# The token list of a mixture-of-experts stage: eight units' row one-hots by one comparison, and ScalarE on the block side of every fourth unit

## The chip, the cores and the metric

The kernel runs on one core of a Trainium2 chip. The metric is the device time of one execution in microseconds (us): the median of the timed runs, lower is better.

## The reference, cut to what matters

One decoder layer on 64 sequences of 256 tokens, 256 features: a quantised self-attention, a cross-attention, and a third block with its own attention and a mixture of eight experts. Only the mixture matters here. T = 16384 tokens; each goes to its two best experts, each expert has C = 4096 places, and a token that comes too late is dropped:

```python
top1 = jnp.argmax(probs, axis=-1)
...
top2 = jnp.argmax(jnp.where(m1 > 0, -jnp.inf, logits), axis=-1)
...
loc1 = jnp.cumsum(m1, axis=0) - 1.0
loc2 = jnp.cumsum(m2, axis=0) - 1.0 + m1.sum(0, keepdims=True)
m1 = m1 * (loc1 < C)
m2 = m2 * (loc2 < C)
...
buf = buf.at[top1, s1].set(x, mode='drop')
buf = buf.at[top2, s2].set(x, mode='drop')
h = jax.nn.relu(jnp.einsum('ecd,edf->ecf', buf, w1) + b1[:, None, :])
```

## The kernel before, in words

The program is a sequence of stages with a barrier of all engines between two of them: `prepare`, three times `attention` (kinds A, X, F), `route`, `dispatch`, `experts`. The stage that the change touches is `dispatch`, some 95 us of the program.

`route` has left, for each of the 128 x 128 tokens (partition p, column n) and each of its two choices i, a slot number between 0 and 32767 (8 experts x 4096 places), split into `high` (slot / 128, 0 to 255) and `low` (slot modulo 128). `dispatch` turns this round: for each slot it finds the token that sits there, as a table `token` of 128 rows x 256 columns, which `experts` reads for its gathers.

It does so by matmuls of one-hot matrices. A **unit** u is one column n and one choice i (n = u // 2, i = u % 2), 256 units in all. For each unit the kernel makes a row side, 128 x 128 in bf16, with a 1 where the column number equals the token's `low`, and a block side, 128 x 256 in bf16, with the token's code where the column number equals its `high`. TensorE multiplies them (row side as the weights, block side as the moving operand of 256 columns) and adds all 256 products in one PSUM tile `code_sum` of 128 x 256.

- VectorE makes both sides of 214 units, with one TENSOR_SCALAR each (L1366 for `by_row`, one comparison; L1367 for `block_of`, a comparison and a product). Each has six buffers, R = 6.
- ScalarE makes both sides of every sixth unit (42 units, SHARE = 6), with two ACTIVATEs for each side: Abs of the distance (`row_gap` L1383, `block_gap` L1384), then Relu of one minus it (`row_a` L1396, `block_a` L1397). Two buffers each, RA = 2. The gaps of the next ScalarE unit are issued ahead of the shapes of this one.
- TensorE takes the units in their number's order (L1411) and waits for each one's sides.
- Before the loop VectorE makes the codes and their negatives, step by step (L1349 to L1359), and turns GpSimd's column numbers (L1342) into bf16 (L1361). ScalarE starts when the thirteenth of these steps is done.
- Behind the loop VectorE waits for the last matmul, copies the sum out (L1370) and makes the token numbers (L1371 to L1374). Then the stage ends.
- The DMA queue of SyncE writes the gates (`tail`) to memory meanwhile (L1336) and waits for that.

The order on each engine is written out by hand; no planner is in it. The lines that bind the engines are:

```python
if d >= R:
    dve.wait_ge(summed, ON_DVE[d - R] + 1)
...
if a >= RA:
    act.wait_ge(summed, ON_ACT[a - RA] + 1)
...
dve.wait_ge(summed, U)
chain.step(v.tensor_copy(codes[:, :], code_sum[:, :]))
```

Of the kernel before, what the change touches and what calls it, by code (L numbers as in the profile page):

```python
# [68 lines left out]
def allocators(nc, ctx, prefix):  # L69
    def sb(name, shape, dtype=F32):  # L70
        return ctx.enter_context(nc.sbuf_tensor(prefix + name, shape, dtype))

    def ps(name, shape, dtype=F32):
        return ctx.enter_context(nc.psum_tensor(prefix + name, shape, dtype))

    sems = []

    def sem(name):
        sems.append(nc.alloc_semaphore(prefix + name))
        return sems[-1]  # L80
# [1224 lines left out]
def dispatch(nc, C, D, io, scratch):  # L1305


    NT, CAP = D["T"] // P, D["CAP"]
    HI = NE * CAP // P
    R, RA = 6, 2  # L1310
    U = 2 * NT
    SHARE = 6
    BIAS = 127 - NT // 2
    with ExitStack() as ctx:
        sb, ps, sem = allocators(nc, ctx, "disp_")
        column, columns = sb("column", [P, HI], I32), sb("columns", [P, HI], BF16)
        place, power = sb("place", [P, NT], I32), sb("power", [P, NT], I32)
        row1, unit = sb("row1", [P, 1]), sb("unit", [P, 1])
        code, code_minus = sb("code", [P, NT]), sb("code_minus", [P, NT])
        low_minus, high_minus = [[sb(f"{n}{i}", [P, NT]) for i in range(2)] for n in ("low_minus", "high_minus")]  # L1320
        by_row, block_of = ([sb(f"{n}{k}", [P, m], BF16) for k in range(R)] for n, m in (("by_row", P), ("block_of", HI)))
        row_gap, block_gap = ([sb(f"{n}{k}", [P, m]) for k in range(RA)] for n, m in (("row_gap", P), ("block_gap", HI)))
        row_a, block_a = ([sb(f"{n}{k}", [P, m], BF16) for k in range(RA)] for n, m in (("row_a", P), ("block_a", HI)))
# [3 lines left out]
        numbered, link, built, spaced, shaped, summed, tail_out = (  # L1327
            sem(n) for n in ("numbered", "link", "built", "spaced", "shaped", "summed", "tail_out"))
        ON_ACT = [u for u in range(U) if u % SHARE == SHARE - 1]
        ON_DVE = [u for u in range(U) if u % SHARE != SHARE - 1]  # L1330
        powers = power[:, :].bitcast(F32)

        with nc.Block() as block:
            @block.sync
            def _(sp):
                sp.dma_start(scratch["h2"].rearrange("(n p) f -> p n f", p=P)[:, :, 256:259], C["tail"][:, :, :],  # L1336
                             allow_slow_non_contiguous=True).then_inc(tail_out, 16)
                sp.wait_ge(tail_out, 16)

            @block.gpsimd  # L1340
            def _(pool):
                nc.gpsimd.iota(column[:, :], [[1, HI]], base=0, channel_multiplier=0).then_inc(numbered, 1)  # L1342
                pool.wait_ge(numbered, 1)

            @block.vector
            def _(dve):
                v = nc.vector
                chain = Chain(dve, link, 0, 18, C["passed"])
                chain.step(v.tensor_scalar(place[:, :], C["number"][:, :], 7, None, ALU.logical_shift_right))  # L1349
                chain.step(v.tensor_scalar(place[:, :], place[:, :], BIAS, None, ALU.add))  # L1350
                chain.step(v.tensor_scalar(power[:, :], place[:, :], 23, None, ALU.logical_shift_left))
                chain.step(v.tensor_copy(row1[:, :], C["number"][:, 0:1]))
                chain.step(v.tensor_scalar(row1[:, :], row1[:, :], 1.0 / P, 1.0, ALU.mult, ALU.add))
                chain.step(v.tensor_scalar(code[:, :], powers, row1[:, :], None, ALU.mult))
                chain.step(v.tensor_scalar(code_minus[:, :], code[:, :], -1.0, None, ALU.mult))
                chain.step(v.memset(unit[:, :], 1.0))
                for i in range(2):
                    chain.step(v.tensor_scalar(low_minus[i][:, :], C["low"][i][:, :], -1.0, None, ALU.mult))
                    chain.step(v.tensor_scalar(high_minus[i][:, :], C["high"][i][:, :], -1.0, None, ALU.mult))  # L1359
                dve.wait_ge(numbered, 1)  # L1360
# [12 lines left out]
                chain.step(v.tensor_scalar(nothing[:, :], number[:, :], 0.0, float(2 ** 20), ALU.is_equal, ALU.mult))  # L1373
                chain.step(v.scalar_tensor_tensor(C["token"][:, :], number[:, :], -float(P * BIAS), nothing[:, :], ALU.add,  # L1374
                                                  ALU.add))
                chain.close()

            @block.scalar
            def _(act):
                def gaps(a):  # L1380
# [7 lines left out]
                gaps(0)  # L1388
                for a, u in enumerate(ON_ACT):
                    n, k = u // 2, a % RA  # L1390
                    if a + 1 < len(ON_ACT):
                        gaps(a + 1)
                    act.wait_ge(spaced, a + 1)
                    if a >= RA:
                        act.wait_ge(summed, ON_ACT[a - RA] + 1)
                    nc.scalar.activation(row_a[k][:, :], row_gap[k][:, :], ACT.Relu, bias=unit[:, :], scale=-1.0)  # L1396
                    nc.scalar.activation(block_a[k][:, :], block_gap[k][:, :], ACT.Relu, bias=code[:, n:n + 1],  # L1397
                                         scale=code_minus[:, n:n + 1]).then_inc(shaped, 1)

            @block.tensor  # L1400
            def _(pe):
                for u in range(U):
                    if u in ON_ACT:
                        a = ON_ACT.index(u)
                        pe.wait_ge(shaped, a + 1)
                        row, blocks = row_a[a % RA], block_a[a % RA]
                    else:
                        d = ON_DVE.index(u)
                        pe.wait_ge(built, d + 1)
                        row, blocks = by_row[d % R], block_of[d % R]  # L1410
                    nc.tensor.matmul(code_sum[:, :], row[:, :], blocks[:, :], start=u == 0, stop=u == U - 1).then_inc(summed, 1)  # L1411

# [554 lines left out]
```

## Time and profile before

| | |
|---|---|
| median of 3 runs | 5688.54 us (5688.51 to 5694.07) |
| profiled execution, its own time | 5689.64 us |
| its span, first to last instruction | 5687.9 us |
| TensorE / VectorE / ScalarE busy, share of the span | 93% / 79% / 65% |
| granted TensorE clock, mean of the span | 0.974 |

"Busy" is the time in which an engine had an instruction running. Matmul records overlap, because matmuls are pipelined and their ends are modelled, so a share of 93% is not 93% of what TensorE can do. In a timeline the start of an instruction is its first number and its duration the second; on VectorE and ScalarE the next instruction can start before the one ahead has ended. "Idle before" is the time that the engine stood still ahead of an instruction, and the name behind the arrow is what ended it. The granted clock is a share of TensorE's full 2.4 GHz: 0.50 is its lower level of 1.2 GHz.

### The profile page before, as it was taken

The numbers are of one execution on the slowest core, as the hardware profiler recorded it, in microseconds if no ns is written. First come the engines' busy times: TensorE is split into PE (matmuls) and PEld (weight loads), VectorE is DVE, ScalarE is ACT, GpSimd is POOL, SyncE is SP. The second block draws the span as 40 slices with busy tenths as digits, with TensorE's granted clock in tenths as the row PEclk, the third lists the DMA queues.
The fourth block names the chain that finished last, engine by engine and source line by source line (L and its number), as shares of the span: only waits on it lengthen the run. The fifth ranks groups of instructions, "written<-read, shape, count | busy, mean of one in ns | idle before, by whom it ended". The sixth has DMA issues, their size and how long they took to land. (4 is left out here: it accounts for less than half of the span.)

```text
span 5687.9 us, 155750 instructions
## 1 busy us (share of the span) xinstructions
PE 5301.0 (93%) x47387; PEld 4213.5 (74%) x47388; DVE 4520.0 (79%) x12198; ACT 3673.0 (65%) x8251; POOL 2070.8 (36%) x1753
## 2 busy tenths in 40 slices
PE   0899999979999999799999999995899999999998
PEld 0677777757777777567777777761799999899997
DVE  7889998867777777588888888878777777677776
ACT  4788888858888888577777776764344444444443
POOL 0322222223344333244444444430344444344443
PEclk9999999989999999999999999995899999999999
DMA  5677777746666666466666666652222322222321
GB/s 157 173 183 184 183 184 183 183 124 185 184 186 184 184 183 186 122 168 180 178 168 180 178 169 178 179 144 6 65 57 42 57 50 44 53 47 43 58 41 26
DMA packets 631736, 751.04 MB, mean 132 GB/s; under 512 B 143363, under 2 KB 560332, under 8 KB 631472
## 3 DMA queue, kind: packets, MB, share of 16 engines
q1 hardware_dynamic: 575136, 679.62, 45.9%
q0 software_dynamic: 49152, 63.10, 6.9%
q10 hardware_dynamic: 7184, 5.00, 0.4%
q8 instruction: 142, 2.33, 0.2%
q14 instruction: 122, 1.00, 0.1%
HBM read 476.49 MB, written 272.24 MB: 132 GB/s over the span
## 5 line engine op out<-in xcount | busy, mean ns | idle before, releaser
L1853 POOL DMA_INDIRECT out_dram<-exp_gated,exp_token x256 | 425.6, 1662 | 890.1 <-DMA out_dram<-exp_gated,exp_token 325.5
L831 ACT ACTIVATE F_probs<-F_scoreT 128x512 f32<-128x512 f32 x1024 | 585.8, 592 | 233.7 <-PE F_scoreT L658 233.3
L940 DVE TENSOR_REDUCE F_tops<-F_score 128x2 f32<-128x512 f32 x1024 | 684.0, 686 | 53.4 <-PE F_score L686 36.3
L940 DVE TENSOR_REDUCE A_tops<-A_score 128x3 f32<-128x384 f32 x1024 | 528.0, 553 | 64.3 <-PE A_score L676 56.3
L831 ACT ACTIVATE A_probs<-A_scoreT 128x384 f32<-128x384 f32 x1024 | 451.1, 488 | 28.7 <-PE A_scoreT L646 15.2
L658 PE MATMUL F_scoreT<-QS,KS 98*128 98x256 bf16 x2048 | 365.5, 275 | 9.7 <-ACT F_probs L831 1.5
L686 PE MATMUL F_score<-KS,QS 96*128 96x256 bf16 x2048 | 362.9, 274 | 8.8 <-DMA KS<-d_k 7.9
L1834 POOL DMA_INDIRECT exp_x<-d_h,exp_token x256 | 281.1, 1098 | 179.3 <-DMA exp_w<-in_L_ffn_w_dram 101.7
L1630 ACT ACTIVATE exp_hT<-exp_hT,exp_b 128x512 f32<-128x512 f32 x512 | 338.6, 711 | 3.1 <-DVE exp_hT L1785 3.1
L940 DVE TENSOR_REDUCE X_tops<-X_score 128x4 f32<-128x484 f32 x512 | 323.4, 653 | 15.7 <-PE X_score L681 14.5
L831 ACT ACTIVATE X_probs<-X_scoreT 121x512 f32<-121x512 f32 x512 | 297.2, 588 | 31.4 <-PE X_scoreT L654 28.6
L671 PE MATMUL A_score<-causal,ident_b 128*128 128x256 bf16 x1024 | 283.7, 277 | 12.4 <-DMA KS<-d_k 8.5
L823 ACT ACTIVATE X_score<-X_mask 128x484 f32<-128x484 bf16 x512 | 288.3, 571 | 8.0 <-DVE X_tops L940 6.8
L642 PE MATMUL A_scoreT<-ident_b,causal 128*128 128x128 bf16 x2048 | 286.6, 221 | 3.1 <-ACT A_probs L831 1.3
L674 PE MATMUL A_score<-KS,QS 96*128 96x256 bf16 x1024 | 281.9, 275 | 0.0
L646 PE MATMUL A_scoreT<-QS,KS 98*128 98x256 bf16 x1024 | 277.7, 271 | 0.0
L712 PE MATMUL F_outs<-F_probs,V 128*32 128x256 f32 x4096 | 275.7, 387 | 1.9 <-ACT F_outT L840 1.9
L1664 ACT ACTIVATE exp_pair<-exp_lead 128x256 f32<-128x256 f32 x256 | 98.3, 384 | 264.7 <-PE exp_lead L1589 264.5
L658 PEld LDWEIGHTS F_scoreT<-QS,KS 98*128 98x128 bf16 x2048 | 164.2, 97 | 134.8 <-issue 51.9
L1655 ACT ACTIVATE exp_lone<-exp_lead 128x256 f32<-128x256 f32 x256 | 98.3, 384 | 242.3 <-PE exp_lead L1574 234.7
L1550 PE MATMUL exp_side_r<-exp_w2s,exp_hTs 128*128 128x128 f32 x2048 | 249.7, 275 | 0.0
L1110 POOL TENSOR_TENSOR A_left_q<-A_q_f,A_q_parts 128x512 f32<-128x512 f32 x64 | 74.1, 1158 | 473.4 <-ACT A_q_parts L905 473.4
(392 smaller groups left out, 16046.8 us busy)
## 6 DMA issues: line engine op xcount, KB each, us to landing
QS<-d_q SPq DMA_DIRECT2D x384, 192.0 KB, 3.7
KS<-d_k SPq DMA_DIRECT2D x256, 192.0 KB, 4.0
QS<-d_q SPq DMA_DIRECT2D x384, 128.0 KB, 3.9
KS<-d_k SPq DMA_DIRECT2D x256, 128.0 KB, 4.0
d_q<-A_q_parts SPq DMA_DIRECT2D x64, 384.0 KB, 3.5
d_k<-A_k_parts SPq DMA_DIRECT2D x64, 384.0 KB, 3.9
QS<-d_q SPq DMA_DIRECT2D x384, 64.0 KB, 3.6
d_q<-X_q_parts SPq DMA_DIRECT2D x64, 384.0 KB, 2.7
```

The costliest lines, as they stand in the source:

```text
L642: mm(s[:, n * P:(n + 1) * P], C["causal"][:, 0:P], ident_b[:, :], start=n == 0, stop=False, skip_group_check=True)
L646: last = mm(s[:, P:384], k[0:98, i, 0:P], q[0:98, i, :], start=False, stop=True, skip_group_check=True)
L658: last = mm(s[:, n * 256:(n + 1) * 256], k[0:98, i, n * P:(n + 1) * P], q[0:98, i, :], start=True, stop=True)
L671: mm(s[:, 0:384].rearrange("p (n k) -> p n k", n=3)[:, 0:3:2, :], ident_b[:, :], C["causal"][:, :].rearrange("p (n k) -> p n k", n=2), sta ...
L674: mm(s[:, P:384], q[0:96, i, P:256], k[0:96, i, :], start=False, stop=False, skip_group_check=True)
L686: last = mm(s[:, n * 256:(n + 1) * 256], q[0:96, i, n * P:(n + 1) * P], k[0:96, i, :], start=True, stop=True)
L823: nc.scalar.activation(score[i % SB][:, 0:2 * HB * KN].rearrange("p (u n k) -> p u n k", u=HB, n=2), mask[gp][:, :, 0:KN].unsqueeze(1).bro ...
L831: nc.scalar.activation(probs[m % 2][0:KR, at:at + HB, :].rearrange("p u x -> p (u x)"), scoreT[i % TB][0:KR, 0:HB * TCOL], ACT.Exp)\
L940: nc.vector.tensor_reduce(dst, src, AX.X, ALU.max).then_inc(score_read, 1)
L1630: nc.scalar.activation(hT[par][:, f, :], hT[par][:, f, :], ACT.Relu, bias=b1[k][:, f:f + 1])\
L1834: nc.gpsimd.indirect_dma_start(x[j % XB][:, s, :], None, scratch["h2"], bass.IndirectOffsetOnAxis(token[j % (2 * XB)][:, s:s + 1], 0), bou ...
L1853: nc.gpsimd.indirect_dma_start(out, bass.IndirectOffsetOnAxis(token[j % (2 * XB)][:, s:s + 1], 0), gated[par][:, s, :], None, bounds_check ...
```

## The change

The row side of eight units (G = 8) is now made by VectorE with one TENSOR_TENSOR comparison. Its first input `repeated` is a constant 128 x 1024 bf16 tile that holds every column number eight times in a row (made once, by a GpSimd iota and a conversion to bf16); its second is the eight units' `low` values, eight adjacent bf16 numbers per partition, read again for each of the 128 column numbers. The output has the eight units interleaved: column j of unit g is element 8 j + g. TensorE therefore reads a unit's weights with a step of 8 elements (16 bytes). There are three such tiles (RR = 3), and 32 such comparisons.

The block side is made per unit as before, by VectorE for 192 units (eight buffers, R = 8) and by ScalarE for every fourth (64 units, SHARE = 4, RA = 3). ScalarE makes no row sides any more. VectorE now waits for `summed` ahead of each comparison of rows and ahead of each block side; before it waited once per unit, ahead of the row side.

```diff
-    R, RA = 6, 2
-    U = 2 * NT
-    SHARE = 6
+    U, G, RR, R, RA = 2 * NT, 8, 3, 8, 3
+    N = U // G
+    SHARE = 4
...
+        spread_out, repeated = sb("spread_out", [P, P, G], I32), sb("repeated", [P, P, G], BF16)
...
+                nc.gpsimd.iota(spread_out[:, :, :], [[1, P], [0, G]], base=0, channel_multiplier=0).then_inc(numbered, 1)
...
-                chain.step(v.memset(unit[:, :], 1.0))
                 for i in range(2):
-                    chain.step(v.tensor_scalar(low_minus[i][:, :], C["low"][i][:, :], -1.0, None, ALU.mult))
+                    chain.step(v.tensor_copy(low[:, :, i], C["low"][i][:, :]))
...
                 chain.step(v.tensor_copy(columns[:, :], column[:, :]))
-                for d, u in enumerate(ON_DVE):
-                    n, i, k = u // 2, u % 2, d % R
-                    if d >= R:
-                        dve.wait_ge(summed, ON_DVE[d - R] + 1)
-                    v.tensor_scalar(by_row[k][:, :], columns[:, 0:P], C["low"][i][:, n:n + 1], None, ALU.is_equal)
-                    v.tensor_scalar(block_of[k][:, :], columns[:, :], C["high"][i][:, n:n + 1], code[:, n:n + 1],
-                                    ALU.is_equal, ALU.mult).then_inc(built, 1)
+                chain.step(v.tensor_copy(repeated[:, :, :], spread_out[:, :, :]))
+                d = 0
+                for k in range(N):
+                    if k >= RR:
+                        dve.wait_ge(summed, G * (k - RR + 1))
+                    lows = low[:, :, :].rearrange("p n i -> p (n i)")[:, G * k:G * k + G].unsqueeze(1).broadcast_to([P, P, G])
+                    v.tensor_tensor(by_row[k % RR][:, :, :], repeated[:, :, :], lows, ALU.is_equal).then_inc(rows_built, 1)
+                    for u in range(G * k, G * k + G):
+                        if u not in ON_DVE:
+                            continue
+                        if d >= R:
+                            dve.wait_ge(summed, ON_DVE[d - R] + 1)
+                        n, i = u // 2, u % 2
+                        v.tensor_scalar(block_of[d % R][:, :], columns[:, :], C["high"][i][:, n:n + 1], code[:, n:n + 1],
+                                        ALU.is_equal, ALU.mult).then_inc(built, 1)
+                        d += 1
...
-                    nc.scalar.activation(row_gap[k][:, :], columns[:, 0:P], ACT.Abs, bias=low_minus[i][:, n:n + 1])
                     nc.scalar.activation(block_gap[k][:, :], columns[:, :], ACT.Abs, bias=high_minus[i][:, n:n + 1])\
                         .then_inc(spaced, 1)
...
-                    nc.scalar.activation(row_a[k][:, :], row_gap[k][:, :], ACT.Relu, bias=unit[:, :], scale=-1.0)
...
                 for u in range(U):
+                    k = u // G
+                    if u % G == 0:
+                        pe.wait_ge(rows_built, k + 1)
...
-                    nc.tensor.matmul(code_sum[:, :], row[:, :], blocks[:, :], start=u == 0, stop=u == U - 1).then_inc(summed, 1)
+                    nc.tensor.matmul(code_sum[:, :], by_row[k % RR][:, :, u % G], blocks[:, :], start=u == 0, stop=u == U - 1)\
+                        .then_inc(summed, 1)
```

VectorE's order at the head of the loop, before; each row is an instruction, with its output and inputs and the output's size:

```order
L1358 TENSOR_SCALAR disp_low_minus<-low 128x128
L1359 TENSOR_SCALAR disp_high_minus<-high 128x128
L1361 CAST disp_columns<-disp_column 128x256
L1366 TENSOR_SCALAR disp_by_row<-disp_columns,low 128x128
L1367 TENSOR_SCALAR disp_block_of<-disp_columns,high,disp_code 128x256
L1366 TENSOR_SCALAR disp_by_row<-disp_columns,low 128x128
L1367 TENSOR_SCALAR disp_block_of<-disp_columns,high,disp_code 128x256
```

and now:

```order
L1358 CAST disp_low<-low 128x128
L1359 TENSOR_SCALAR disp_high_minus<-high 128x128
L1361 CAST disp_columns<-disp_column 128x256
L1362 CAST disp_repeated<-disp_spread_out 128x1024
L1368 TENSOR_TENSOR disp_by_row<-disp_repeated,disp_low 128x1024
L1375 TENSOR_SCALAR disp_block_of<-disp_columns,high,disp_code 128x256 x6
L1368 TENSOR_TENSOR disp_by_row<-disp_repeated,disp_low 128x1024
L1375 TENSOR_SCALAR disp_block_of<-disp_columns,high,disp_code 128x256 x6
```

A comparison of 1024 elements and six block sides have taken the place of the pairs, and one conversion of 1024 elements stands ahead of the loop.

ScalarE's order in the loop, before:

```order
L1383 ACTIVATE disp_row_gap<-disp_columns,disp_low_minus 128x128
L1384 ACTIVATE disp_block_gap<-disp_columns,disp_high_minus 128x256
L1396 ACTIVATE disp_row_a<-disp_row_gap,disp_unit 128x128
L1397 ACTIVATE disp_block_a<-disp_block_gap,disp_code,disp_code_minus 128x256
```

and now:

```order
L1392 ACTIVATE disp_block_gap<-disp_columns,disp_high_minus 128x256 x2
L1404 ACTIVATE disp_block_a<-disp_block_gap,disp_code,disp_code_minus 128x256
L1392 ACTIVATE disp_block_gap<-disp_columns,disp_high_minus 128x256
L1404 ACTIVATE disp_block_a<-disp_block_gap,disp_code,disp_code_minus 128x256
```

Two ACTIVATEs per ScalarE unit are left of four.

## Rows read from the trace of the kernel before

**Rows 1.** Busy time by stretch: in `route`, and the loop of `dispatch`

```profile
core 0: us, PE busy (x) PEld busy (x) DVE busy (x) ACT busy (x) POOL busy (x), PEclk, DMA share, GB/s
3873.00:3903.00 30.00, 2.25 (x5) 0.61 (x5) 26.64 (x63) 1.25 (x2) 0.00 (x0) 0.50 0.00 0
...
3907.40:3997.61 90.21, 85.71 (x256) 23.37 (x256) 89.72 (x428) 70.35 (x168) 0.00 (x0) 0.50 0.36 2
```

**Rows 2.** Waits, 3903 to 4002 us: us in total, times, longest

```profile
PEld disp_code_sum L1411 <- DVE disp_block_of L1367: 71.4, 214, 5.4
...
ACT disp_row_a L1396 <- PE disp_code_sum L1411: 13.7, 35, 1.2
```

**Rows 3.** Waits of the SyncE queue in the same stretch

```profile
SPq L1333 <- PEq L1333: 71.3, 1, 71.3
...
SPq L1333 <- DMA d_h<-tail: 24.1, 1, 24.1
```

**Rows 4.** Instructions on the row and block tiles: ns min/median/max, first and last start

```profile
L1366 DVE TENSOR_SCALAR disp_by_row<-disp_columns,low x214: 234/236/255, 3907.4 to 3996.6; 128x128 bf16<-128x128 bf16 x107
L1411 PEld LDWEIGHTS disp_code_sum<-disp_block_of,disp_by_row x214: 101/103/106, 3908.0 to 3997.2; 128*128 128x128 bf16 x107
...
L1367 DVE TENSOR_SCALAR disp_block_of<-disp_columns,high,disp_code x214: 327/329/341, 3907.6 to 3996.8; 128x256 bf16<-128x256 bf16 x107
```

**Rows 5.** Timeline of VectorE in the middle of the loop: start us, us

```profile
3950.13 0.23 DVE L1366 TENSOR_SCALAR disp_by_row<-disp_columns,low 128x128 bf16<-128x128 bf16 x1
3950.30 0.33 DVE L1367 TENSOR_SCALAR disp_block_of<-disp_columns,high,disp_code 128x256 bf16<-128x256 bf16 x1
3950.55 0.24 DVE L1366 TENSOR_SCALAR disp_by_row<-disp_columns,low 128x128 bf16<-128x128 bf16 x1
```

**Rows 6.** Groups by line, VectorE: busy us, mean ns of one

```profile
L1276 DVE TENSOR_SCALAR route_pos<-route_pos 128x128 f32<-128x128 f32 x1 | 0.2, 226 | 0.0
...
L1280 DVE TENSOR_TENSOR route_slot<-route_pos,route_base 128x128 f32<-128x128 f32 x1 | 0.3, 291 | 0.0
...
L1274 DVE TENSOR_TENSOR route_loc<-route_loc,route_one 128x1024 f32<-128x1024 f32 x2 | 2.5, 1225 | 0.1
...
L944 DVE COPY X_maskT<-X_mask 128x244 bf16<-128x244 bf16 x64 | 13.9, 218 | 0.0
```

**Rows 7.** Timeline of VectorE, two comparable instructions behind each other in `experts`

```profile
4010.60 0.68 DVE L1703 TENSOR_TENSOR exp_w1s<-exp_w 128x512 f32<-128x512 f32 x1
4011.20 0.68 DVE L1705 TENSOR_TENSOR exp_w1s<-exp_w1s,exp_w 128x512 f32<-128x512 f32 x1
```

**Rows 8.** Timeline ahead of the loop, at its start and at its end

```profile
3903.96 0.35 POOL L1342 IOTA disp_column<- 128x256 int32 x1 [49.91 <-POOLq L84]
...
3905.93 0.06 DVE L1356 MEMSET disp_unit<- 128x1 f32 x1
...
3907.40 0.26 DVE L1366 TENSOR_SCALAR disp_by_row<-disp_columns,low 128x128 bf16<-128x128 bf16 x1
...
3996.80 0.33 DVE L1367 TENSOR_SCALAR disp_block_of<-disp_columns,high,disp_code 128x256 bf16<-128x256 bf16 x1
3997.61 0.42 DVE L1370 COPY disp_codes<-disp_code_sum 128x256 f32<-128x256 f32 x1 [0.49 <-PE disp_code_sum L1411]
```

**Rows 9.** Timeline of ScalarE at the start of the loop

```profile
3908.40 0.49 ACT L1384 ACTIVATE disp_block_gap<-disp_columns,disp_high_minus 128x256 f32<-128x256 bf16 x1
3908.80 0.39 ACT L1396 ACTIVATE disp_row_a<-disp_row_gap,disp_unit 128x128 bf16<-128x128 f32 x1
...
3909.09 0.58 ACT L1397 ACTIVATE disp_block_a<-disp_block_gap,disp_code,disp_code_minus 128x256 bf16<-128x256 f32 x1
...
3909.71 0.40 ACT L1383 ACTIVATE disp_row_gap<-disp_columns,disp_low_minus 128x128 f32<-128x128 bf16 x1
```

**Rows 10.** Timeline of TensorE in `route`: matmuls of 512 columns, and a weight load

```profile
3873.93 0.64 PE L1225 MATMUL route_whole<-route_one,ones_b 128*128 128x512 bf16 x1
3874.36 0.64 PE L1224 MATMUL route_inside<-route_one,below 128*128 128x512 bf16 x1
...
3874.36 0.15 PEld L1225 LDWEIGHTS route_whole<-route_one,ones_b 128*128 128x128 bf16 x1 [0.28 <-issue]
```

More of the change, by code:

```diff
@@ L1316, in dispatch @@
         column, columns = sb("column", [P, HI], I32), sb("columns", [P, HI], BF16)
+        spread_out, repeated = sb("spread_out", [P, P, G], I32), sb("repeated", [P, P, G], BF16)
         place, power = sb("place", [P, NT], I32), sb("power", [P, NT], I32)
[L1318 to L1323, printed above, removed]
+        row1, code, code_minus = sb("row1", [P, 1]), sb("code", [P, NT]), sb("code_minus", [P, NT])
+        low, high_minus = sb("low", [P, NT, 2], BF16), [sb(f"high_minus{i}", [P, NT]) for i in range(2)]
+        by_row = [sb(f"by_row{k}", [P, P, G], BF16) for k in range(RR)]
+        block_of = [sb(f"block_of{k}", [P, HI], BF16) for k in range(R)]
+        block_gap, block_a = ([sb(f"{n}{k}", [P, HI], t) for k in range(RA)] for n, t in (("block_gap", F32), ("block_a", BF16)))
         codes, number, nothing = sb("codes", [P, HI]), sb("number", [P, HI]), sb("nothing", [P, HI])
@@ L1326, in dispatch @@
         code_sum = ps("code_sum", [P, HI])
-        numbered, link, built, spaced, shaped, summed, tail_out = (
-            sem(n) for n in ("numbered", "link", "built", "spaced", "shaped", "summed", "tail_out"))
+        numbered, link, rows_built, built, spaced, shaped, summed, tail_out = (
+            sem(n) for n in ("numbered", "link", "rows_built", "built", "spaced", "shaped", "summed", "tail_out"))
         ON_ACT = [u for u in range(U) if u % SHARE == SHARE - 1]
@@ L1342, in _ @@
                 nc.gpsimd.iota(column[:, :], [[1, HI]], base=0, channel_multiplier=0).then_inc(numbered, 1)
-                pool.wait_ge(numbered, 1)
+                nc.gpsimd.iota(spread_out[:, :, :], [[1, P], [0, G]], base=0, channel_multiplier=0).then_inc(numbered, 1)
+                pool.wait_ge(numbered, 2)
             @block.vector
@@ L1355, in _ @@
                 chain.step(v.tensor_scalar(code_minus[:, :], code[:, :], -1.0, None, ALU.mult))
-                chain.step(v.memset(unit[:, :], 1.0))
                 for i in range(2):
-                    chain.step(v.tensor_scalar(low_minus[i][:, :], C["low"][i][:, :], -1.0, None, ALU.mult))
+                    chain.step(v.tensor_copy(low[:, :, i], C["low"][i][:, :]))
                     chain.step(v.tensor_scalar(high_minus[i][:, :], C["high"][i][:, :], -1.0, None, ALU.mult))
-                dve.wait_ge(numbered, 1)
+                dve.wait_ge(numbered, 2)
                 chain.step(v.tensor_copy(columns[:, :], column[:, :]))
-                for d, u in enumerate(ON_DVE):
-                    n, i, k = u // 2, u % 2, d % R
-                    if d >= R:
-                        dve.wait_ge(summed, ON_DVE[d - R] + 1)
-                    v.tensor_scalar(by_row[k][:, :], columns[:, 0:P], C["low"][i][:, n:n + 1], None, ALU.is_equal)
-                    v.tensor_scalar(block_of[k][:, :], columns[:, :], C["high"][i][:, n:n + 1], code[:, n:n + 1],
-                                    ALU.is_equal, ALU.mult).then_inc(built, 1)
+                chain.step(v.tensor_copy(repeated[:, :, :], spread_out[:, :, :]))
[14 more added lines that the diff above has]
+                        d += 1
                 dve.wait_ge(summed, U)
@@ L1379, in _, with gap @@
             def _(act):
-                def gaps(a):
+                def gap(a):
                     n, i, k = ON_ACT[a] // 2, ON_ACT[a] % 2, a % RA
                     need(act, shaped, a - RA + 1)
-                    nc.scalar.activation(row_gap[k][:, :], columns[:, 0:P], ACT.Abs, bias=low_minus[i][:, n:n + 1])
                     nc.scalar.activation(block_gap[k][:, :], columns[:, :], ACT.Abs, bias=high_minus[i][:, n:n + 1])\
@@ L1387, in _ @@
                 act.wait_ge(link, 13)
-                gaps(0)
+                gap(0)
                 for a, u in enumerate(ON_ACT):
@@ L1391, in _ @@
                     if a + 1 < len(ON_ACT):
-                        gaps(a + 1)
+                        gap(a + 1)
                     act.wait_ge(spaced, a + 1)
@@ L1405, in _ @@
                         pe.wait_ge(shaped, a + 1)
-                        row, blocks = row_a[a % RA], block_a[a % RA]
+                        blocks = block_a[a % RA]
                     else:
@@ L1409, in _ @@
                         pe.wait_ge(built, d + 1)
-                        row, blocks = by_row[d % R], block_of[d % R]
-                    nc.tensor.matmul(code_sum[:, :], row[:, :], blocks[:, :], start=u == 0, stop=u == U - 1).then_inc(summed, 1)
+                        blocks = block_of[d % R]
+                    nc.tensor.matmul(code_sum[:, :], by_row[k % RR][:, :, u % G], blocks[:, :], start=u == 0, stop=u == U - 1)\
+                        .then_inc(summed, 1)
 def experts(nc, C, D, io, scratch, out):
```

## The prediction
> **What bounds the kernel now.** The change touches one stage, so I read that stage and not the whole program. First the busy times by stretch [rows 1]: in the loop of `dispatch`, 3907.40 to 3997.61 us, VectorE is busy for 89.72 of 90.21 us. ScalarE is at 70.35 us, and GpSimd does nothing. TensorE's 85.71 us look as full as VectorE's, but its records overlap; the waits decide [rows 2]. TensorE's weight loads waited 214 times, once for each of VectorE's units, 71.4 us in total, for the block side. ScalarE stood 13.7 us waiting for TensorE to give back a buffer. So VectorE's instruction stream is the bound, and TensorE follows it.
>
> Does the stage end with the loop? The SyncE queue shows it [rows 3]: its write of the gates landed after 24.1 us, and it then waited 71.3 us for the other engines at the stage's end. The next stage starts behind the barrier, so a microsecond taken from the loop is one taken from the time, until the stage has lost some 70 of them.
>
> Inside VectorE's stream [rows 4, 5]: a row side starts, the block side starts 0.17 us later, the next row side 0.25 us later. That is 0.42 us per unit, and 214 x 0.42 = 89.9 us, the loop. An instruction starts some 0.07 to 0.08 us before the one ahead has ended (0.236 against 0.17, 0.329 against 0.25). Between a block side and the next row side stands the wait for `summed`, and the step is no longer for it.
>
> **Price of the new comparison.** 32 TENSOR_TENSORs of 1024 elements with both inputs and the output in bf16. No row shows a two-input instruction on bf16 inputs. With f32 inputs, 1024 elements take 1.225 us and 128 take 0.291 [rows 6]: 1.04 ns per element, and 0.158 us whatever the size. One-input instructions: 128 f32 elements take 0.226 us, 0.53 ns per element above 0.158; 244 bf16 elements take 0.218 us, 0.25 ns per element. So bf16 halves the price of an element there. If it does so with two inputs too, the comparison takes 0.158 + 1024 x 0.52 = 0.69 us. The bounds are 1.225 us (nothing halved) and 0.158 + 1024 x 0.25 = 0.41 us (as cheap as a bf16 copy). I take 0.69: the f32 rows have two inputs at half the rate of one, so the same ratio against bf16's 0.25 gives 0.5 too. Its next instruction starts after 0.61 us, as two of 0.68 us do [rows 7] that start 0.60 apart.
>
> The Trainium skill's page "VectorE: DVE Perf Modes", section "The perf-mode tier table", gives a bf16 tensor_tensor in SBUF two elements per cycle, and "Vector Engine (DVE) Microarchitecture Reference", section 5.1, says that an input row read again and again still ran so. By these pages the comparison is an estimated 0.69 us as well; no run here shows it.
>
> **The sum.** A group of eight units on VectorE is one comparison and six block sides (the other two are ScalarE's): 0.61 + 6 x 0.255 = 2.14 us. The block sides now follow each other with a wait between any two; the step of 0.25 us above already has a wait in it [rows 5], so I charge nothing for it. 32 groups give 68.5 us, the last block side starting 0.26 us before that. From the last block side to the copy of the sum it was 0.81 us [rows 8]; now ScalarE's unit 255 comes behind it, one more matmul of 0.21 us. So start of the loop to the copy: 68.5 - 0.26 + 0.81 + 0.21 = 69.3 us, where it was 90.2.
>
> Ahead of the loop: a memset goes (0.06 us and its step's 0.04), two products become two conversions of the same size (nothing), and the conversion of 1024 int32 elements comes, one input at 0.53 ns per element: 0.158 + 0.54 = 0.70, with its step 0.73 us. Net +0.63 us. GpSimd's second iota has four times the elements of the first, which took 0.35 us [rows 8]; at four times that it ends at 3903.96 + 0.35 + 1.4 = 3905.7, and VectorE asks for it at 3907. Hidden. If GpSimd were ten times slower than that, it would show.
>
> Sum: 69.3 + 0.6 = 69.9 us in place of 90.2, **20.3 us less**. The profiled execution took 5689.64 us (span 5687.9), so 5669.3 by its measure; it lies 1.1 us above the median of the runs, and against the median 5688.54 the sum is **5668.2 us**.
>
> **What must keep up.** ScalarE: a distance is followed by the next instruction after 0.40 us, a block shape of 0.58 us after 0.62 us where a wait on its own result follows (the drop from two buffers), some 0.50 where none does [rows 9]. With RA = 3 no ScalarE instruction waits for the one just ahead, so a ScalarE unit costs 0.90 us, at worst 1.02, and VectorE gives it half a group, 1.07 us. Covered, with 0.05 to 0.17 us to spare: the thinnest cover in the change.
>
> TensorE: the clock stands at 0.50, 1.2 GHz, through `route` and the loop [rows 1]. There matmuls of 512 columns with a weight load for each start 0.43 us apart, 0.83 ns per column, the load inside the matmul ahead [rows 10]. For 256 columns that is 0.213 us per unit, 1.71 us per group against 2.14. Covered. Nothing becomes late for the buffers: VectorE's eighth block buffer was used ten units (2.7 us) earlier.
>
> **Rivals.**
>
> *The comparison runs at one element per cycle* (the change does not do what it says). Then it costs 1.225 - 0.08 = 1.14 us, a group 2.67, the loop 85.5 + 0.8, with the 0.6 ahead 86.9: 3.3 us less, 5685.2. For it: no bf16 row with two inputs, and an input pattern of eight elements repeated 128 times. Against it: bf16's halving in the one-input rows. 0.07.
>
> *The weights become the bound, and it is slower.* Weights are now read with a step of 16 bytes; all loads of this stage so far are of adjacent elements, 0.103 us each [rows 4]. The load hides behind a matmul of 0.213 us. If it takes longer than 0.27 us, TensorE, not VectorE, sets the group (8 x 0.267 = 2.14); from (90.2 - 1.6) / 256 = 0.35 us on, the change loses. At four times today's load, 0.41 us, the loop is 256 x 0.41 = 105.5, with start and head 107.2: +17 us, 5705.5. Nearest rows are only the contiguous loads, and the lower bound is no change at all. The Trainium skill, "SBUF — State Buffer", section "Specifications (TRN2)", speaks against this change: SBUF's lines are 16 bytes, full bandwidth needs two hits per line, and here every column is in a line of its own. At half the rate by that rule the load is an estimated 0.21 us and still hides. No row here shows a strided load. Slower: 0.05.
>
> *ScalarE or TensorE bounds it a little.* Each ScalarE instruction waiting for the one ahead: (0.49 + 0.04) + (0.58 + 0.04) = 1.15 us per four units, 64 x 1.15 = 73.6, with start, end and head 75.4: 14.8 us less, 5673.7. A weight load plus a part of the matmul at 0.30 us per unit: 76.8 + 2 = 78.8, 11.4 less, 5677. Or the waits between block sides end the overlap on VectorE: 0.33 a piece, a group of 2.59 us, 5682. Together 0.10.
>
> **How the numbers follow.** The forecast, a gain of 18 to 22 us, has 0.78. I take 5668. Its own bounds: block sides at 0.25 to 0.27 us each move it by 1 to 3 us, and the first comparison's price by little; the three runs before spread upwards by 5.5 us. The range reaches into the third rival and leaves out the first two and the 0.41 us bound of the comparison (-9 us), since two inputs at the price of one contradict the f32 rows: 5663 to 5680. A change of 0.2% is 11.4 us, about what a measurement of this kernel can tell from no change. The forecast and most of the third rival are faster; the one-element comparison and the last form of the third rival are within it; the weights are slower. Faster 0.87, same 0.08, slower 0.05.
>
> **What the profile will show.** If right: the loop, first comparison to copy of the sum, 68 to 71 us; L1368 at 0.69 us, L1375 starting 0.25 to 0.26 us apart, VectorE busy for all of it; TensorE's loads waiting for VectorE, not the other way; ScalarE with waits of its own; the clock at 0.50 or at most higher. L1368 at 1.2 us is the first rival. Weight loads well over 0.11 us, and VectorE waiting for `summed`, are the second. A TensorE that waits for `block_a` is the third. The prediction as a whole is wrong if the loop shortens and the stages behind it, which the change does not touch, give the time back.

## The result and the profile after

| | before | changed |
|---|---|---|
| median of 6 runs | 5691.01 us | 5671.17 us (5668.46 to 5674.28) |
| ratio, 95% interval | 1 | 0.9965 (0.9952 to 0.9978) |
| span of the profiled execution | 5687.9 us | 5671.4 us |
| `dispatch`: VectorE's first instruction to the loop | 3.42 us | 5.16 us |
| `dispatch`: loop, first row side to copy of the sum | 90.21 us | 69.37 us |

The medians are 19.8 us apart, the forecast was 20.3 from the sum. The changed kernel's time lies in the range of 5663 to 5680, 3 us above the forecast 5668.2; the median of the kernel before also came out 2.5 us higher over six runs than over the first three.

The stretch ahead of the changed loop, and then the loop, by the table of stretches (columns as in [rows 1]):

```profile
3911.35:3916.51 5.16, 0.00 (x0) 0.00 (x0) 4.71 (x14) 0.00 (x1) 1.69 (x2) 0.50 0.92 13
3916.51:3985.88 69.37, 55.13 (x256) 32.14 (x256) 68.83 (x225) 60.13 (x128) 0.00 (x0) 0.84 0.45 3
```

VectorE is busy for 68.83 of 69.37 us, as it was before [rows 1]; the number of its instructions in the loop fell from 428 to 224 (and one at the edge). ScalarE's share rose from 78 to 87%. TensorE's granted clock, 0.50 all through the loop before, is 0.84 on the mean.

The timeline of VectorE at the head of the loop (start, duration, then the instruction; "x6" is six of them merged) carries the prices, against [rows 5]:

```profile
3915.78 0.69 DVE L1362 CAST disp_repeated<-disp_spread_out 128x1024 bf16<-128x1024 int32 x1
3916.51 0.69 DVE L1368 TENSOR_TENSOR disp_by_row<-disp_repeated,disp_low 128x1024 bf16<-128x1024 bf16 x1
3917.11 1.62 DVE L1375 TENSOR_SCALAR disp_block_of<-disp_columns,high,disp_code 128x256 bf16<-128x256 bf16 x6
3918.64 0.69 DVE L1368 TENSOR_TENSOR disp_by_row<-disp_repeated,disp_low 128x1024 bf16<-128x1024 bf16 x1
```

The comparison takes 0.69 us, the first block side starts 0.60 us after it, six block sides step in 3918.64 - 3917.11 = 1.53 us, 0.255 each. A group is 2.13 us where the sum had 2.14.

The waits in the stretch (in total, times, longest), against [rows 2] and [rows 3]:

```profile
PEld disp_code_sum L1421 <- DVE disp_by_row L1368: 29.3, 32, 7.7
PE disp_code_sum L1421 <- DVE disp_block_of L1375: 20.6, 32, 7.5
ACT disp_block_a L1404 <- PE disp_code_sum L1421: 6.7, 21, 0.7
```

```profile
SPq L1333 <- PEq L1333: 51.8, 1, 51.8
...
SPq L1333 <- DMA d_h<-tail: 24.6, 1, 24.6
```

TensorE waits for VectorE once in each of the 32 groups; ScalarE still stands 6.7 us for buffers; no wait of VectorE's inside the loop is listed (its one wait, 0.5 us, is for the last matmul). The write of the gates has 51.8 us to spare at the stage's end, 19.5 less than before.

What the forecast did not have is ahead of the loop. VectorE and GpSimd at the start of the stage:

```profile
3911.32 0.35 POOL L1342 IOTA disp_column<- 128x256 int32 x1 [49.91 <-POOLq L84]
3911.35 0.40 DVE L1350 TENSOR_SCALAR disp_place<-number 128x128 int32<-128x128 int32 x1 [0.98 <-PEq L84]
3911.63 1.41 POOL L1343 IOTA disp_spread_out<- 128x1024 int32 x1
3911.78 1.33 DVE L1351 TENSOR_SCALAR disp_place<-disp_place 128x128 int32<-128x128 int32 x1
3913.15 0.23 DVE L1352 TENSOR_SCALAR disp_power<-disp_place 128x128 int32<-128x128 int32 x1
```

L1351 is an instruction of 128 elements like its neighbour L1352, 0.23 us, and it took 1.33. It ended at 3913.11, GpSimd's second iota at 3913.04.

One caution for all that follows: the stage does not start at the same time in every execution. In the profiled executions VectorE's first instruction of `dispatch` lies between 3903.9 and 3917.7 us, 3903.98 in that of the kernel before, 3911.35 in that of the changed one, although nothing in front of it differs. Single times therefore scatter by more than the effects below, and the experiments are read by the stage's own two stretches.

### The profile page after: what moved, and what is told of

Its sections match the earlier page's. It is cut to its first block and busy times, and to the rows that moved or that the text cites. A ratio compares the mean times of both kernels' runs of the same rounds, so it can differ in the third digit from the quotient of the medians.

```text
span 5671.4 us, 155561 instructions
## 1 busy us (share of the span) xinstructions
PE 5267.9 (93%) x47388; PEld 4218.4 (74%) x47388; DVE 4506.5 (79%) x11994; ACT 3661.2 (65%) x8211; POOL 2071.3 (37%) x1754
```

## The experiments

Loop and head (first instruction to first row side) of each run, from the starts in the timelines of VectorE. The granted clock is that of the loop.

| run | head us | loop us | clock | time us (kernel before, measured beside it) |
|---|---|---|---|---|
| before | 3.42 | 90.21 | 0.50 | 5691.01, median of six |
| changed | 5.16 | 69.37 | 0.84 | 5671.17 (5691.01), medians of six |
| e1, rows compared in f32 | 5.13 | 86.54 | 0.50 | 5690.98 (5695.74) |
| e3, no second iota | 4.05 | 69.28 | 0.85 | 5679.87 (5695.74) |
| e4, ScalarE every sixth | 5.15 | 74.86 | 0.73 | 5687.02 (5695.74) |
| e5, adjacent weights | 5.15 | 69.07 | 0.86 | 5669.62 (5689.23) |
| e6, kernel before, ScalarE every fourth | 3.43 | 103.78 | 0.50 | 5706.26 (5689.23) |
| e7, four units | 5.10 | 71.34 | 0.95 | 5677.40 (5689.23) |
| e8, sixteen units | 6.55 | 68.08 | 0.81 | 5667.98 (5689.23) |
| e9, second iota twice | 7.00 | 69.31 | 0.85 | 5680.65 (5697.81) |
| e10, two units in seven | 3.32 | 66.94 | 0.93 | 5670.34 (5697.81) |
| e11, changed kernel again | 5.16 | 69.44 | 0.87 | 5674.08 (5694.01) |
| e12, e10's kernel again | 3.33 | 67.08 | 0.86 | 5668.69 (5694.01) |

e1 and e3 to e9 are single times, e10 to e12 medians of five. e2, e5's edit without the two copies that e5 adds behind the loop, has no time.

### e1: what bf16 on both inputs is worth

```diff
-... sb("repeated", [P, P, G], BF16)
+... sb("repeated", [P, P, G])
-        low, high_minus = sb("low", [P, NT, 2], BF16), ...
+        low, high_minus = sb("low", [P, NT, 2]), ...
```

> Both inputs of the row comparison are f32 instead of bf16 (output bf16 as before); nothing else is changed. Theory A (VectorE's instruction stream bounds the loop, and the bf16 inputs let the comparison take two elements per cycle): L1368 goes from 0.69 us, its first and undisturbed duration, to 1.22 us, the group of eight units from 2.14 to 2.67 us, and the loop (first comparison to copy of the sum) from 69.4 to 86 to 87 us. Theory B (TensorE with its strided weight loads holds the pace): the group is 2.14 us for TensorE's reasons, so part of the 0.53 us is hidden, and the loop stays below 80 us.

Measured: one time of 5690.98 us beside 5695.74 of the kernel before. The comparison by its tile (ns min/median/max):

```profile
L1368 DVE TENSOR_TENSOR disp_by_row<-disp_repeated,disp_low x32: 1208/1214/1224, 3916.1 to 3999.1; 128x1024 bf16<-128x1024 f32 x32
```

1.21 us each, a loop of 86.54 us, inside theory A's 86 to 87. All of the 0.53 us per group came through to the loop, so nothing else was holding the pace. It is also the first rival with its condition made true: had the bf16 comparison run at one element per cycle, the loop would have shortened by 3.7 us and the head cost 1.7.

### e4 and e6: the two halves of the change, each alone

e4 keeps the packed rows and gives ScalarE its old share. e6 is the kernel before with the new share alone.

```diff
-    SHARE = 4
+    SHARE = 6
```

> Only ScalarE's share is put back to every sixth unit: 42 block sides by ScalarE, 214 by VectorE; the packed comparison stays. Theory A (VectorE bounds): 32 x 0.61 + 214 x 0.256 = 74.3 us, the loop 74.9 to 75.3 us, so the packing alone is worth some 15 of the loop's 20.8 us and the share 5.6. Theory B (TensorE holds the pace at 0.2 us or more per unit): the 22 more block sides on VectorE are partly hidden, the loop below 73 us.

Measured: the loop 74.86 us. Packing the rows is worth 90.21 - 74.86 = 15.4 us, the share on top of it 5.5. The 15.4 us include that VectorE now compares the rows of ScalarE's units too, and the new numbers of buffers, which e4 keeps.

```diff
-    SHARE = 6
+    SHARE = 4
```

> The kernel before with one number changed: ScalarE makes both sides of every fourth unit instead of every sixth. VectorE has 192 pairs of 0.42 us, 80.6 us. Theory S (ScalarE must keep up, and four ACTIVATEs of 1.62 us per unit do not fit in three pairs of 1.26 us): ScalarE bounds, 64 x 1.62 = 104 us, the loop 104 to 106 us in place of 90.2, TensorE's waits are for block_a, VectorE waits for summed. Theory A alone (VectorE's stream sets the loop whatever ScalarE does): the loop is 81 to 82 us.

Measured: 5706.26 us beside 5689.23 of the kernel before. The waits of e6:

```profile
PEld disp_code_sum L1411 <- ACT disp_block_a L1397: 66.7, 64, 1.1
...
PE disp_code_sum L1411 <- ACT disp_block_a L1397: 36.6, 63, 0.6
...
DVE disp_by_row L1366 <- PE disp_code_sum L1411: 15.6, 58, 0.3
```

and its loop by the table of stretches:

```profile
3912.20:4015.98 103.78, 66.55 (x256) 27.63 (x256) 85.70 (x384) 101.21 (x256) 0.00 (x0) 0.50 0.32 2
```

ScalarE is busy for 101.21 of 103.78 us, and TensorE waited 64 times for its block side, once per ScalarE unit. So the same number, SHARE = 4, costs 13.6 us alone and gains 5.5 together with the packed rows. A ScalarE unit costs 103.78 / 64 = 1.62 us in e6, where the pairs of three VectorE units last 1.26; with two ACTIVATEs it costs 0.90, where half a group lasts 1.07.

### e5: do the strided weight loads hold the pace?

```diff
+                for h in range(2):
+                    chain.step(v.tensor_copy(C["token"][:, h * NT:h * NT + NT], C["number"][:, :]))
...
-... by_row[k % RR][:, :, u % G], blocks[:, :], ...
+... by_row[k % RR][:, :, :].rearrange("p c g -> p (c g)")[:, P * (u % G):P * (u % G) + P], blocks[:, :], ...
```

> TensorE reads each unit's weights as 128 adjacent elements of the row tile instead of 128 elements with a step of 16 bytes. The sum in PSUM is then not the token list, so behind the loop two copies (some 0.5 us) put a fixed list in its place, in which no slot is empty; times behind the loop are not compared. Theory A (VectorE's stream bounds the loop): the weight loads fall from 0.143 us to about 0.10, and the loop, first comparison to copy of the sum, stays at 69.4 us within 0.3. Theory B (the strided loads hold the pace): the loads fall likewise and the loop gets shorter by more than 1 us.

The weight loads of VectorE's units, first in the changed kernel, then in e5:

```profile
L1421 PEld LDWEIGHTS disp_code_sum<-disp_block_of,disp_by_row x192: 140/143/148, 3917.6 to 3985.4; 128*128 128x128 bf16 x192
```

```profile
L1423 PEld LDWEIGHTS disp_code_sum<-disp_block_of,disp_by_row x192: 95/96/106, 3910.1 to 3977.7; 128*128 128x128 bf16 x192
```

e5 does not read the one-hots of its units: its sum is not the token list, and the two copies put a fixed list in its place. Only its loop is therefore compared, not its total.

The step of 16 bytes costs each load 0.047 us by its record (0.143 against 0.096 at about the same clock), 12 us over 256 loads, and the loop went from 69.37 to 69.07 us. The last comparison and the copy of the sum, first in the changed kernel, then in e5:

```profile
3982.72 1.07 DVE L1368 TENSOR_TENSOR disp_by_row<-disp_repeated,disp_low 128x1024 bf16<-128x1024 bf16 x1
...
3985.88 0.42 DVE L1379 COPY disp_codes<-disp_code_sum 128x256 f32<-128x256 f32 x1 [0.54 <-PE disp_code_sum L1421]
```

```profile
3975.44 0.67 DVE L1368 TENSOR_TENSOR disp_by_row<-disp_repeated,disp_low 128x1024 bf16<-128x1024 bf16 x1
...
3978.14 0.42 DVE L1379 COPY disp_codes<-disp_code_sum 128x256 f32<-128x256 f32 x1 [0.49 <-PE disp_code_sum L1423]
```

From the first comparison to the last it is 66.21 us in the changed kernel and 66.37 in e5: the pace is the same. The loop's difference lies behind the last comparison, 3.16 against 2.70 us, and part of that is not due to the loads either, since in e9, with strided loads, it is 2.86. Theory B is out.

### e7 and e8: four and sixteen units per comparison

```diff
-    U, G, RR, R, RA = 2 * NT, 8, 3, 8, 3
+    U, G, RR, R, RA = 2 * NT, 4, 6, 8, 3
```

> The comparison covers four units (512 elements, 64 of them, six row tiles), so weights have a step of 8 bytes. Theory A with a fixed price per instruction: each comparison 0.158 + 512 x 0.52 = 0.42 us, the next instruction after 0.345; 64 x 0.345 + 192 x 0.256 = 71.2, the loop 72.0 us, 2.6 more than with eight. If the price went by elements alone the loop would stay at 69.4. Weight loads: if what makes them slow is a new 16-byte line per column, they fall from 0.143 us towards 0.10; if any step above one does it, they stay at 0.14.

```diff
-    U, G, RR, R, RA = 2 * NT, 8, 3, 8, 3
+    U, G, RR, R, RA = 2 * NT, 16, 2, 8, 3
```

> The comparison covers sixteen units (2048 elements, 16 of them, two row tiles), so weights have a step of 32 bytes. Theory A: each comparison 1.22 us, the next after 1.145; 16 x 1.145 + 192 x 0.256 = 67.5, the loop 68.3 us, 1.1 less than with eight. Theory B (TensorE's loads): with loads at or above 0.17 us the loop is not shorter than 69.4. Ahead of the loop: the second iota has 2048 elements, 2.8 us, VectorE's held instruction 2.7 us, and the conversion 1.22 us: 5.16 + 1.4 + 0.5 = 7.1 us to the first comparison.

The loads and comparisons of e7, then of e8:

```profile
L1421 PEld LDWEIGHTS disp_code_sum<-disp_block_of,disp_by_row x192: 110/113/118, 3916.6 to 3986.7; 128*128 128x128 bf16 x192
...
L1368 DVE TENSOR_TENSOR disp_by_row<-disp_repeated,disp_low x64: 407/414/426, 3915.8 to 3985.5; 128x512 bf16<-128x512 bf16 x64
```

```profile
L1421 PEld LDWEIGHTS disp_code_sum<-disp_block_of,disp_by_row x192: 140/143/167, 3912.6 to 3978.6; 128*128 128x128 bf16 x192
...
L1368 DVE TENSOR_TENSOR disp_by_row<-disp_repeated,disp_low x16: 1211/1215/1226, 3911.0 to 3974.3; 128x2048 bf16<-128x2048 bf16 x16
```

The loop is 71.34 us with four units, 69.37 with eight, 68.08 with sixteen, against 72.0, 69.3 and 68.3 worked out. Comparisons of 512, 1024 and 2048 elements take 0.414, 0.69 and 1.215 us: 0.52 ns per element on a fixed 0.15. About half of the fixed part is hidden, since the next instruction starts before the comparison ends: 32 comparisons more cost the loop 1.97 us, 0.06 each, and 16 fewer saved 1.29, 0.08 each. Four units are the middle case for the loads: 0.113 us with a step of 8 bytes, between 0.096 (adjacent) and 0.143 (16 bytes); 32 bytes cost no more than 16. So the load gets dearer up to a step of 16 bytes and no further; no run shows why. The rule of the Trainium skill that the prediction cited (lines of 16 bytes, two hits in each for the full rate) fits the steps of 16 and 32 bytes, with one column in a line; at 8 bytes, with two, it has no loss, and 0.017 us was measured. A load's record does not depend on its step alone: in e6, with adjacent weights, the same loads have a median of 0.151 us. The shorter loop of e8 is eaten at its head, 6.55 us (7.1 had been expected; the iota of 2048 elements took 2.27 us, not 2.8).

### e3 and e9: what held L1351

```diff
-                nc.gpsimd.iota(spread_out[:, :, :], [[1, P], [0, G]], base=0, channel_multiplier=0).then_inc(numbered, 1)
...
-                chain.step(v.tensor_copy(repeated[:, :, :], spread_out[:, :, :]))
+                chain.step(v.tensor_copy(repeated[:, :, :], columns[:, 0:P].unsqueeze(2).broadcast_to([P, P, G])))
```

(The waits that count the iotas, one fewer, are left out here.)

> The tile of repeated column numbers is made by VectorE alone, from the bf16 column numbers read eight times each; GpSimd's second iota of 1024 elements is gone. Theory P (VectorE's L1351 took 1.33 us instead of 0.23 because it could not run until GpSimd's iota was through; both want SBUF at the same time): L1351 (place) is back at 0.23 us, and the stretch from VectorE's first instruction of the stage to the first comparison falls from 5.16 to 4.06 us. Theory Q (something else at the stage's start holds VectorE, such as the write of the gates): L1351 stays at 1.3 us and the stretch at 5.2. The conversion stays at 0.69 us in both (two elements per cycle), the loop at 69.4.

e9 keeps the iota and issues it a second time behind the first:

```diff
-                nc.gpsimd.iota(spread_out[:, :, :], [[1, P], [0, G]], base=0, channel_multiplier=0).then_inc(numbered, 1)
-                pool.wait_ge(numbered, 2)
+                for n in range(2):
+                    nc.gpsimd.iota(spread_out[:, :, :], [[1, P], [0, G]], base=0, channel_multiplier=0).then_inc(numbered, 1)
+                    pool.wait_ge(numbered, 2 + n)
...
-                dve.wait_ge(numbered, 2)
+                dve.wait_ge(numbered, 3)
```

> GpSimd runs the iota of 1024 elements twice in a row, the second behind the first; VectorE waits for both where it waited for one (that wait is 4 us later). Theory P (a VectorE instruction is held while GpSimd's iota runs): VectorE loses another 1.1 to 1.2 us, in one of the instructions behind L1351 or in a longer L1351, and the stretch to the first comparison is 6.3 us in place of 5.16. Theory Q (the 1.1 us comes once, from the stage's start or the write of the gates): the stretch stays at 5.2 us.

The head of e3 by the timeline:

```profile
3916.37 0.40 DVE L1349 TENSOR_SCALAR disp_place<-number 128x128 int32<-128x128 int32 x1 [0.98 <-PEq L84]
3916.80 0.23 DVE L1350 TENSOR_SCALAR disp_place<-disp_place 128x128 int32<-128x128 int32 x1
```

and that of e9, VectorE and then GpSimd:

```profile
3915.38 1.33 DVE L1352 TENSOR_SCALAR disp_place<-disp_place 128x128 int32<-128x128 int32 x1
3916.74 2.07 DVE L1353 TENSOR_SCALAR disp_power<-disp_place 128x128 int32<-128x128 int32 x1
```

```profile
3915.22 3.51 POOL L1344 IOTA disp_spread_out<- 128x1024 int32 x2
```

Without the iota the same instruction takes 0.23 us and the head 4.05 us, 1.11 less; that is 3.42 + 0.63, the head that the prediction had. With a second iota the next VectorE instruction is held too, 2.07 us in place of 0.23, and ends at 3918.81 where GpSimd's pair ends at 3918.73. The direction is theory P's; the size is not, since the second iota took 3.51 - 1.41 = 2.1 us in place of 1.4, and the head came to 7.00 us in place of 6.3. Theory Q is out. That it is access to SBUF that the two share is theory P's reading of it; the runs show that VectorE's instruction ends 0.07 to 0.09 us after GpSimd's does, for iotas of 1.41, 1.61 (e7) and 2.27 us (e8). e7, where the iota is longer though its tile is smaller, shows it best:

```profile
3911.00 1.61 POOL L1343 IOTA disp_spread_out<- 128x512 int32 x1
3911.15 1.54 DVE L1351 TENSOR_SCALAR disp_place<-disp_place 128x128 int32<-128x128 int32 x1
```

The Trainium skill's page "Advanced Engine Details and Errata", section "GPSIMD Details", states that GpSimd shares a read and a write interface with VectorE and conflicts with its two-port instructions. The rows fit that, but none shows whether the held instruction used two ports.

### e10, e11 and e12: a version that does more of the same

The second iota is gone, ScalarE makes the repeated tile (one ACTIVATE, Copy, of 1024 elements) while VectorE makes the codes, and ScalarE has two units in seven. For that VectorE converts the column numbers as its fourth step and not at the end of the head.

```diff
-        ON_ACT = [u for u in range(U) if u % SHARE == SHARE - 1]
-        ON_DVE = [u for u in range(U) if u % SHARE != SHARE - 1]
+        ON_ACT = [u for u in range(U) if u % 7 in (3, 6)]
+        ON_DVE = [u for u in range(U) if u % 7 not in (3, 6)]
...
+                dve.wait_ge(numbered, 1)
+                chain.step(v.tensor_copy(columns[:, :], column[:, :]))
...
-                chain.step(v.tensor_copy(columns[:, :], column[:, :]))
-                chain.step(v.tensor_copy(repeated[:, :, :], spread_out[:, :, :]))
...
-                act.wait_ge(link, 13)
+                act.wait_ge(link, 4)
+                nc.scalar.activation(repeated[:, :, :], columns[:, 0:P].unsqueeze(2).broadcast_to([P, P, G]), ACT.Copy)\
+                    .then_inc(numbered, 1)
+                act.wait_ge(link, 12)
```

> A version that should beat both: ScalarE makes the block side of two units in seven (73) instead of one in four (64), and it also makes the tile of repeated column numbers while VectorE makes the codes; GpSimd's second iota is gone. Theory A: VectorE 32 x 0.61 + 183 x 0.256 = 66.4 us, ScalarE 73 x 0.90 = 65.7 us plus its start and end, so the loop 67 to 68.5 us; the stretch ahead of it 3.4 us in place of 5.16. Together 3 to 4 us less than the changed kernel, some 22 to 24 less than the kernel before: ratio 0.9960. If ScalarE's instructions cost their full 1.15 us per unit because they wait for each other, ScalarE bounds and the loop is 84 us.

> The changed kernel itself once more, beside the next one on the same chip. The loop 69.3 to 69.4 us, the stretch ahead of it 5.16; some 19 to 20 us less than the kernel before, ratio 0.9965. The stages in front of it, which the change does not touch, put the start of the stage anywhere from 3904 to 3918 us, as in the runs so far, so single times scatter by more than the loop does.

> The version with ScalarE on two units in seven and the repeated tile on ScalarE once more, beside the changed kernel: by the stage's own times (66.9 and 3.4 us against 69.4 and 5.16) 4.2 us less than the changed kernel, ratio to it 0.9993, which these rounds may or may not separate. If it is not less at all, the stages behind give it back.

e10: 5670.34 us over five runs, 0.9951 of the kernel before (0.9938 to 0.9965). In the last pair, on one chip beside each other: the changed kernel 5674.08 us, 0.9965 (0.9951 to 0.9979), this version 5668.69 us, 0.9952 (0.9938 to 0.9965). ScalarE's head and the loop by the timeline and the table of stretches of e12:

```profile
3914.00 1.06 ACT L1395 ACTIVATE disp_repeated<-disp_columns 128x1024 bf16<-128x1024 bf16 x1 [29.05 <-DVE disp_columns L1353]
3916.04 0.91 ACT L1391 ACTIVATE disp_block_gap<-disp_columns,disp_high_minus 128x256 f32<-128x256 bf16 x2 [0.98 <-DVE disp_high_minus L1360]
```

```profile
3916.04:3983.12 67.08, 53.90 (x256) 32.53 (x256) 66.54 (x215) 65.22 (x146) 0.00 (x0) 0.86 0.59 3
```

The tile is made with 0.98 us to spare, VectorE and ScalarE are both nearly full (66.54 and 65.22 of 67.08 us), and head and loop together are 70.4 us where the changed kernel has 74.6. The 4.2 us show in the stage in both profiles and as 5.4 us between the medians; the intervals of the two ratios overlap, so the total alone does not separate them. Both beat the kernel before by more than the intervals.

## Why the prediction was right, and where it was not

**The bound.** VectorE's stream, as the busy time and TensorE's waits had it [rows 1, 2]. Every edit of that stream moved the loop by what it adds or removes: e1 +17.2, e4 +5.5, e7 +2.0, e8 -1.3, e10 -2.4 us, each loop within 0.7 us of the one worked out, at clocks from 0.50 to 0.95. The edit of TensorE's side moved it by 0.3 (e5), all of it behind the last comparison.

**The comparison's price.** 0.69 us taken, 0.69 measured. The halving by bf16 that two one-input rows suggested [rows 6] holds with two inputs, and eight elements read again 128 times don't break it. The tier table and section 5.1 of the Trainium skill's pages that the prediction cited agree.

**The block sides back to back.** A wait between any two was charged at nothing because [rows 5] had one inside the 0.25 us step. 0.255 measured.

**The loop.** 69.3 us predicted, 69.37 measured, 69.44 in e11. Its parts came out too: from the first comparison to the last 66.3 us by the sum (31 x 2.14), 66.21 measured; from there to the copy 2.9 by the sum, 3.16 measured.

**The head: the step that failed.** The prediction wrote of GpSimd's second iota: "at four times that it ends at 3903.96 + 0.35 + 1.4 = 3905.7, and VectorE asks for it at 3907. Hidden." Its length came out (1.41 us), but by luck: it was scaled by the number of elements, and e7's tile of half as many took 1.61, e8's of twice as many 2.27. VectorE did not wait for its result. But the iota cost 1.1 us by holding an instruction that has nothing to do with it: head +1.74 us in place of +0.63. A hint of it stood in the trace of before, where VectorE's first instruction took 0.40 us beside the first iota of 0.35 [rows 8], and the like ones behind it 0.23:

```profile
3903.98 0.40 DVE L1349 TENSOR_SCALAR disp_place<-number 128x128 int32<-128x128 int32 x1 [0.98 <-PEq L84]
3904.42 0.23 DVE L1350 TENSOR_SCALAR disp_place<-disp_place 128x128 int32<-128x128 int32 x1
```

It ends 0.07 us after that iota, as the held ones do; no run leaves the first iota out, so that this too is a hold is not shown. A cover was looked for only on the wait, not on the neighbour.

**ScalarE.** 0.90 us per unit was taken; the first ones step 0.90 (block shapes at 3917.32, 3918.22, 3919.11 in its timeline), with 6.7 us of waits for buffers left over. In e12, with 73 units, it is busy 65.22 of 67.08 us, and still VectorE's sum holds.

**TensorE.** Covered, but with less room than was said: the load is 0.143 us, not 0.103. The rule of the Trainium skill that the prediction set against the change ("SBUF — State Buffer", "Specifications (TRN2)") agrees with e5 and e8 in its direction, has no loss where e7 measured 0.017 us, and its price is off the path. The prediction's estimate was 0.21 us, at half the rate; measured is 0.143. Why it is less than half the rate would give was not tested.

**The rivals.** One element per cycle: excluded by L1368, and priced by e1. Weights: their loads are slower by 0.04 to 0.05 us and not four times as long, and hidden (e5). ScalarE or TensorE a little: no wait of VectorE's in the loop. The end of the overlap between block sides: they step 0.255 us, not 0.33.

**The total.** By the stage, head and loop are 93.63 - 74.53 = 19.1 us less, 19.8 by the medians. The profiled executions differ by 16.5 in span, because the stage began 7.4 us later and the stages behind the loop took 4.8 us less; e11 and e12 show the same kind of scatter in stages that are the same in all kernels.

## What to carry to other kernels

Where one engine's stream of small instructions is the bound and the other engines wait for it, the loop is the sum of start-to-start steps. Here eight row sides as instructions of their own stepped 8 x 0.17 = 1.36 us and one comparison for all eight 0.61; that was worth 15.4 us, the share moved to ScalarE 5.5. Moving a share is worth something only while the helper's time per unit fits in the time it frees: the same number lost 13.6 us with four ACTIVATEs per unit and gained 5.5 with two. For work put on GpSimd as "hidden", look at what VectorE does in the same microseconds, not only at who waits for the result.

## What the runs showed of the hardware that was not expected

- A VectorE TENSOR_SCALAR of 128 int32 elements beside a GpSimd iota ends just after the iota does: 1.33 us in place of 0.23 beside one of 1024 elements, 1.54 beside one of 512 (e7), 2.20 beside one of 2048 (e8), 2.07 beside the second of e9. Other VectorE instructions did not stand beside a long one.
- An iota's time does not follow its elements alone: 1.41 us for 128 x 8, 1.61 for 128 x 4 (e7), 2.27 for 128 x 16 (e8). The count of 512 took longer than that of 1024.
- Weight loads of 128 bf16 columns (medians of VectorE's units): 0.096 us adjacent in e5, 0.113 with a step of 8 bytes, 0.143 with 16 and with 32; adjacent ones had 0.103 in the kernel before and 0.151 in e6.
- TensorE's granted clock was 0.50 through the loops of the kernel before, of e1 and of e6, and on the mean 0.73 to 0.95 in the others. No loop's time needs it to be explained: all follow VectorE's or ScalarE's sum.
- In the changed kernel the recorded durations in the loop grow, L1368 from 0.693 to 1.068 us and L1375 from 0.341 to 0.737, while their starts keep their step; in e9, with the same loop of 69.3 us, they stay at 0.67 to 0.69 and 0.33 to 0.35. The growth is not in the records alone: TensorE's first load of the last group starts 1.45 us after that group's comparison starts in the changed kernel (recorded 1.07 us) and 1.05 us after it in e9 (0.68), some 0.37 us behind the recorded end in both. Prices were therefore read from starts. Why the ends lag stays open.
